# Cross- and self-attention layer: the maxima in one pair of banks with one VectorE instruction for each pair, and a third bank for the projections

## What is computed

```python
x = _layernorm(tgt, ln1_g, ln1_b)
qkv = x @ sa_wqkv
q, k, v = (_heads(t) for t in jnp.split(qkv, 3, axis=-1))
wei = jnp.einsum('bhtd,bhsd->bhts', q, k) * scale
wei = jnp.where(causal[None, None], wei, NEG_INF)
wei = jnp.where(tgt_padding_mask[:, None, None, :], NEG_INF, wei)
wei = jax.nn.softmax(wei, axis=-1)
sa_out = _merge(jnp.einsum('bhts,bhsd->bhtd', wei, v)) @ sa_wproj + sa_bproj
result = tgt + sa_out
xq = _layernorm(result, ln2_g, ln2_b)
xs = _layernorm(src, ln2_g, ln2_b)
kv = xs @ ed_wkv
k2, v2 = (_heads(t) for t in jnp.split(kv, 2, axis=-1))
q2 = _heads(xq @ ed_wq)
wei2 = jax.nn.softmax(jnp.einsum('bhtd,bhjd->bhtj', q2, k2) * scale, axis=-1)
ed_out = _merge(jnp.einsum('bhtj,bhjd->bhtd', wei2, v2)) @ ed_wproj + ed_bproj
result = result + ed_out
h = jax.nn.relu(_layernorm(tgt, ln3_g, ln3_b) @ ff_w1 + ff_b1)
result = result + (h @ ff_w2 + ff_b2)
```

## Time and profile before

| | |
|---|---|
| median of 3 runs | 609.78 us (607.84 to 613.45) |
| the profiled execution | 610.33 us |
| its span, first to last instruction | 608.3 us |
| mean granted TensorE clock | 0.979 of full speed |
| TensorE busy | 551.4 us (91%) |
| VectorE busy | 402.9 us (66%) |
| ScalarE busy | 330.6 us (54%) |
| GpSimd busy | 110.1 us (18%) |

### The profile page before, as it was taken

How to read it: one execution, slowest core, us unless ns; L and a number is a source line. 1 busy time by engine, 2 the same in 40 slices (tenths; PEclk the granted TensorE clock), 3 DMA queues, 4 the chain that set the end, 5 groups by cost and what they waited for, 6 DMA issues and landing times.

```text
span 608.3 us, 14162 instructions
## 1 busy us (share of the span) xinstructions
PE 551.4 (91%) x5564; PEld 445.1 (73%) x5564; DVE 402.9 (66%) x982; ACT 330.6 (54%) x615; POOL 110.1 (18%) x367
## 2 busy tenths in 40 slices
PE   3999877999999989899999999899999999999896
PEld 3887765768877877768877777768877777768674
DVE  7943767797477747696478747697568654685571
ACT  5626444266546746267546755357545665375183
POOL 2002312031023112031113112032113111130010
PEclk9869988999999999999999999999999999999998
DMA  8896077593650177392660168393570138104900
GB/s 234 172 133 121 20 118 112 84 116 70 121 123 1 46 107 114 69 127 57 121 135 6 46 84 122 66 123 62 115 119 13 32 81 135 35 3 89 125 2 16
DMA packets 74210, 52.84 MB, mean 87 GB/s; under 512 B 21984, under 2 KB 73376, under 8 KB 74144
## 3 DMA queue, kind: packets, MB, share of 16 engines
q1 hardware_dynamic: 74144, 51.94, 51.3%
HBM read 14.36 MB, written 1.84 MB: 27 GB/s over the span
## 4 chain that ended last, share of the span: by engine, by line
PE 72%; DVE 13%; ACT 8%; issue 3%; POOL 3%; DMA 1%; SPq 0%; DVEq 0%; POOLq 0%; ACTq 0%
PE misc L1142 9%; PE misc L978 9%; PE pvb L1113 9%; PE misc L980 7%; PE misc L979 7%; PE scb L1097 7%; PE mxb L1081 5%; PE misc L1149 5%; DVE negm L885 3%; DVE rem L819 2%; ACT prob L747 2%; PE misc L1120 2%; PE mxb L1078 2%; PE scb L1092 2%; PE misc L1034 2%
## 5 line engine op out<-in xcount | busy, mean ns | idle before, releaser
L747 ACT ACTIVATE prob<-scb 125x448 f32<-125x448 f32 (+1 forms) x256 | 134.8, 544 | 72.1 <-PE scb L1097 68.6
L885 DVE TENSOR_REDUCE negm<-mxb 112x1 f32<-112x375 f32 x256 | 129.4, 540 | 30.0 <-PE mxb L1081 28.8
L1081 PE MATMUL mxb<-k2st,q2st 96*112 96x375 bf16 x256 | 82.0, 338 | 5.7 <-DVE negm L885 5.4
L1097 PE MATMUL scb<-q2st,k2st 128*125 128x112 bf16 x768 | 74.7, 223 | 3.2 <-ACT prob L747 2.1
L1097 PEld LDWEIGHTS scb<-q2st,k2st 128*125 128x125 bf16 x768 | 65.7, 137 | 15.8 <-ACT prob L747 7.9
L819 DVE SCALAR_TENSOR_TENSOR rem<-misc,bcol,qkp 128x224 f32<-128x224 f32 (+2 forms) x64 | 37.5, 586 | 57.2 <-ACT qkp L732 57.0
L678 POOL CAST mparts<-negm 112x8 bf16<-112x8 f32 x64 | 12.5, 195 | 320.8 <-DVE negm L882 175.3
L1142 PE MATMUL misc<-wf,hT 128*112 128x256 f32 x256 | 60.6, 382 | 5.0 <-DVE rem L819 5.0
L1113 PE MATMUL pvb<-prob,v 125*17 125x112 f32 (+1 forms) x2048 | 65.0, 261 | 0.1
L732 ACT ACTIVATE qkp<-misc,bcol 128x224 bf16<-128x224 f32 (+2 forms) x64 | 35.8, 559 | 51.1 <-PE misc L980 51.1
L882 DVE TENSOR_REDUCE negm<-mxb 112x4 f32<-112x448 f32 x64 | 39.2, 616 | 29.1 <-PE mxb L1078 28.9
(11 more groups left out here) (150 smaller groups left out, 1160.6 us busy)
## 6 DMA issues: line engine op xcount, KB each, us to landing
k2st<-qkp SPq DMA_DIRECT2D x192, 93.8 KB, 4.3
xs<-in_ctx SPq DMA_DIRECT2D x16, 375.0 KB
q1st<-qkp SPq DMA_DIRECT2D x48, 112.0 KB, 5.2
k1st<-qkp SPq DMA_DIRECT2D x48, 112.0 KB, 6.6
q2st<-qkp SPq DMA_DIRECT2D x96, 56.0 KB, 2.3
xn<-in_x SPq DMA_DIRECT2D x4, 448.0 KB, 8.0
tb<-in_x SPq DMA_DIRECT2D x8, 224.0 KB, 10.6
out<-ostage SPq DMA_DIRECT2D x16, 112.0 KB, 3.7
```

The source lines that it names most:

```text
L747: nc.scalar.activation(prob[0:rows, n % PROB_SLOTS, :], scb[n % SCORE_BANKS][0:rows, 0:GH * T], ACT.Exp, scale=SCALE).then_inc(s_ex, 1)
L885: V.tensor_reduce(negm[:, at, i:i + 1], mx[0:T, 0:S], axis=AX_X, op=ALU.max, negate=True).then_inc(s_mx, 1)
L1081: mm = M(mx[0:T, 0:S], q2st[0:NROW, i, b * T:(b + 1) * T], k2st[k2_place(q, b)][0:NROW, i, 0:S], start=True, stop=True)
L1097: mm = M(sc[0:rows, j * T:(j + 1) * T], ks, (q1st if u < BG else q2st)[:, h, b * T:(b + 1) * T], start=(u >= BG), stop=(u >= BG or j == GH ...
```

## The change

The three banks `mxb0` to `mxb2` become one tensor `mxb` of two banks, and `misc` gets the third. A `max` step is now a pair: two heads of a cross unit, one in each bank, or twice four heads of a self unit. TensorE fills both banks and signals once; VectorE reduces both with one instruction, over 2 x 375 or 2 x 4 x 112 columns. TensorE's wait is for the reduce of the pair directly before. The quarters' lists follow: a quarter that had four cross maxima has two pairs; the self maxima of quarters g and g + 1 become one pair in the odd quarter, and `max_parts` follows as before.

```diff
-MISC_BANKS, MAX_BANKS, SCORE_BANKS = 2, 3, 2
+MISC_BANKS, SCORE_BANKS = 3, 2
...
     def maxima(u, g):
-        heads = [g] if u < BG else range(4 * g, 4 * g + 4)
-        return [[("max", u, i)] for i in heads] + ([[("max_parts", u, g // 2)]] if g % 2 else [])
+
+        pairs = range(2 * g, 2 * g + 2) if u >= BG else [g // 2] if g % 2 else []
+        return [[("max", u, i)] for i in pairs] + ([[("max_parts", u, g // 2)]] if g % 2 else [])
...
-    opening = [("v1", 0, 0), ("ff1", 0, 2 * kt), ("max", 0, 0, 0), ("max", 0, 0, 1), ("max_parts", 0, 0, 0), ("v1", 0, 1), ("ff1", 0, 2 * kt + 1),
-               ("mT", 0, 0, 0), ("v1", 0, 2), ("ff1", 0, 2 * kt + 2), ("max", 0, 0, 2), ("load_src", 0, 0), ("max", 0, 0, 3), ("max_parts", 0, 0, 1),
-               ("score", 0, 0, 0, 0), ("max", 0, 1, 0), ("score", 0, 0, 1, 0), ("max", 0, 1, 1), ("max_parts", 0, 1, 0), ("v1", 0, 3),
+    opening = [("v1", 0, 0), ("ff1", 0, 2 * kt), ("max", 0, 0, 0), ("max_parts", 0, 0, 0), ("v1", 0, 1), ("ff1", 0, 2 * kt + 1),
+               ("mT", 0, 0, 0), ("v1", 0, 2), ("ff1", 0, 2 * kt + 2), ("load_src", 0, 0), ("max", 0, 0, 1), ("max_parts", 0, 0, 1),
+               ("score", 0, 0, 0, 0), ("max", 0, 1, 0), ("score", 0, 0, 1, 0), ("max_parts", 0, 1, 0), ("v1", 0, 3),
                ("mT", 0, 0, 1), ("ff1", 0, 2 * kt + 3)]
...
-        mxb = [ps(f"mxb{i}", [P, 512]) for i in range(MAX_BANKS)]
+        mxb = ps("mxb", [P, 2, 512])
...
                     if u < BG:
-                        V.tensor_reduce(negm[:, at, i * GH:(i + 1) * GH], mx[0:T, 0:GH * T].rearrange("p (h s) -> p h s", h=GH),
-                                        axis=AX_X, op=ALU.max, negate=True).then_inc(s_mx, 1)
+                        into, of = negm[:, at, i * HH:(i + 1) * HH], mxb[0:T, :, 0:GH * T].rearrange("p a (h s) -> p a h s", h=GH)
                     else:
-                        V.tensor_reduce(negm[:, at, i:i + 1], mx[0:T, 0:S],
-                                        axis=AX_X, op=ALU.max, negate=True).then_inc(s_mx, 1)
+                        into, of = negm[:, at, 2 * i:2 * i + 2], mxb[0:T, :, 0:S]
+                    V.tensor_reduce(into, of, axis=AX_X, op=ALU.max, negate=True).then_inc(s_mx, 1)
...
-                    after(pe, s_mx, before_in(maxes, s, MAX_BANKS))
-                    m, first = divmod(i * (GH if u < BG else 1), HH)
+                    after(pe, s_mx, before_in(maxes, s, 1))
+                    m, first = divmod(i * (HH if u < BG else 2), HH)
...
+                    for a in range(2):
+                        mx = mxb[:, a, :]
+                        if u < BG:
...
+                            for j in range(GH):
+                                h = i * HH + a * GH + j
...
+                        else:
+                            h = 2 * i + a
+                            mm = M(mx[0:T, 0:S], q2st[0:NROW, h, b * T:(b + 1) * T], k2st[k2_place(q, b)][0:NROW, h, 0:S], start=True, stop=True)
                     mm.then_inc(s_mxf, 1)
```

More of the change, by code:

```diff
@@ L367, in layer_kernel @@
         misc = [ps(f"misc{i}", [P, 512]) for i in range(MISC_BANKS)]
-        mxb = [ps(f"mxb{i}", [P, 512]) for i in range(MAX_BANKS)]
+        mxb = ps("mxb", [P, 2, 512])
         scb = [ps(f"scb{i}", [P, 512]) for i in range(SCORE_BANKS)]
         pvb = ps("pvb", [P, 512])
-        qk_bank, vcol_bank, col_bank, row_bank, f1_bank = scb[0], scb[1], pvb, scb[0], mxb[0]
+        qk_bank, vcol_bank, col_bank, row_bank, f1_bank = scb[0], scb[1], pvb, scb[0], mxb[:, 0, :]
         s_w = [sem(f"{w}_landed") for w in ("wqkv", "wkv", "wq2", "wff1")]
@@ L675, in pool_part @@
                     parts = mparts[n % 2]
-                    after(pool, s_mx, ("max", q, u, 2 * half + 1 if u < BG else (half + 1) * HH - 1))
+                    after(pool, s_mx, ("max", q, u, half if u < BG else (half + 1) * HH // 2 - 1))
                     after(pool, s_full, before_in(halves, ("mT", q, u, half), 2))
@@ L875, in dve_part @@
                     u, i = s[2:]
-                    mx = mxb[maxes.index(s) % MAX_BANKS]
                     at = units.index((q, u)) % 2
@@ L1072, in pe_part @@
                         after(pe, s_k2st[b][m], ("stack_k2", q, b, m))
[L1073 to L1081, removed]
+                    for a in range(2):
+                        mx = mxb[:, a, :]
+                        if u < BG:
+                            M(mx[0:T, 0:GH * T].rearrange("p (h s) -> p h s", h=GH), maskt[:, b, :],
+                              identb[0:T, :].unsqueeze(1).broadcast_to([T, GH, T]), start=True, stop=False)
+                            for j in range(GH):
+                                h = i * HH + a * GH + j
+                                mm = M(mx[0:T, j * T:(j + 1) * T], q1st[0:NROW, h, b * T:(b + 1) * T], k1st[0:NROW, h, b * T:(b + 1) * T],
+                                       start=False, stop=(j == GH - 1))
+                        else:
+                            h = 2 * i + a
+                            mm = M(mx[0:T, 0:S], q2st[0:NROW, h, b * T:(b + 1) * T], k2st[k2_place(q, b)][0:NROW, h, 0:S], start=True, stop=True)
                     mm.then_inc(s_mxf, 1)
```

## The result

The changed kernel takes 638.8 us (median of four runs, 636.53 to 639.49) against 608.8 us before: 1.046 times as long, 95% interval 1.041 to 1.050. The direction was forecast, the size not: 30 us where 13 were forecast, above the range's end at 636. The kernel before was timed again beside the experiments, with medians of 609.5, 610.5 and 610.1 us, so a difference between two kernels of different sets is good to a us or two.

What follows compares the result with a forecast made beforehand. TensorE's in-order stream, busy 91% of the span, was taken as the bound. 50 us lost at pairs less 37 taken away (24 third `misc` bank, 6 mT, 7 old `mxb` waits) gave +13 on 609.78: 623 us, range 606 to 636.

Steps and rivals of the forecast that it cites:

- The cycle: From one maxima pair's fill to the next: fill, VectorE start, reduce of 0.93 us, release; 1.51 us in all.
- the sum: The forecast's account over the whole kernel: 50 us lost on pairs less 37 us taken away, +13 us.
- the third `misc` bank: Removes TensorE's waits for readers of misc banks: 22 us (11 to 32) plus 2 us at the ends, 24.
- Rival (a): Break-even, 611 us, chance 0.27: late reduce and misc bank wait share one cause and can't both be paid.
- The ring's rows behind the 22: 20 lines of TensorE load waits for misc bank readers, 95 to 580 us: 32.1 us in 65 waits, taken as 22.
- Of the four groups: 4 x 12.1: Stalls at cross pairs: 7.0 us a group from little work between, 5.1 from late VectorE; 48 us over four groups.
- the 1.19 us: Part of the 1.51 us from pair to pair that must be filled with other TensorE work.
- The self pairs cost nothing: Self pairs come once in two quarters, over 5 us of TensorE work apart, covering their 1.5 us; cost nothing.
- 10 to 24: VectorE time saved, in us, by 160 reduces instead of 320; counts only where a matmul waits behind VectorE's queue.
- Rival (b): Faster, 599 us, chance 0.1: VectorE's queue is the hidden pacer and its full 24 us come back.
- Rival (c): Worse, 635 us, chance 0.13: each of 60 pairs costs 0.2 us more, +12, as stalls push VectorE's work back.
- The rule that was weighed: Rotate matmul groups through banks; break up unsaturated VectorE's instructions where it causes bubbles. By it alone, +37 us.

## Why the prediction was right or wrong

**Right: what a pair costs where it stalls.** The cycle was put at 1.51 us and is 1.51 to 1.56. The reduce was put at 0.93 us and is 0.935. The waits of one group (119.39 to 262.30 us) in the changed kernel:

```profile
PE mxb L1082 <- DVE negm L885: 9.4, 15, 1.5
PE scb L1098 <- ACT prob L748: 2.5, 6, 0.6
```

9.4 us in 15 waits, and with the 0.17 us by which a matmul's row outlasts the distance to the next one (0.33 less 0.16), 15 x 0.17 = 2.5 more, is 11.9 us; the sum had 12.1 for a group, at 15 places. The long one was named too: 1.50 us at the second pair of (3, 3), put at 1.7.

**Right in total, in part by luck: the third `misc` bank.** Put at 24, measured 24.3 with pairs and 18.0 without. Rival (a), that it can't be paid beside the stalls, falls with it. In the traces the steady part gives 19.2 us, not 22, and the start 7.9, not 2. The start's share is unsure: kernels with the same steps up to there reach the first group's unit 3 at 91.44 and 93.59 us with three banks and at 99.34 and 96.24 with two, so it is 3 to 8 us. The ring's rows behind the 22 also lack one of 1.0 us (L978 for `xsT_lo`). mT's matmuls waited 4.7 us for `mparts` and now wait 1.0, where the sum took 6 off.

**Wrong: "Of the four groups: 4 x 12.1".** This is the step that failed by most. The end of the last group was costed like any other. There, the order is the same but the fillers are of a group that doesn't exist, so the work that fills the 1.19 us isn't there; nor are there ring waits to be gained. The end and the last unit 3 lose 16.4 us together, against 8 for two steady groups; up to the last unit 3 the traces are only 9.8 us apart, where the forecast's 13 us would have made about 9. Spreading unit 6's maxima takes 7.2 of it away, and keeping TensorE at work shows that part of it is clock, which no term of the sum held.

**Wrong: "The self pairs cost nothing".** The cover named was the distance from one self pair to the next. The next user of the banks behind the self pair of (2, 3) is a cross pair, 0.39 us of TensorE's work later. The kernels with and without self pairs are 7 us apart, of which the stricter wait at the first maximum of a cross unit has a part (0.45 us a group where it was seen).

**Left out: what stood between the score tiles.** A step of maxima was also what separated two score tiles, long enough for the exponential to free a bank of `scb`. With half as many steps, the tiles wait: 2.5 us a group in matmul rows, 8.2 us in all by the kernel with three score banks.

**Too small, the other way:** one instruction in place of two was given no worth of its own, and the kernel that undoes it is 11 us slower (5 to 18), of which about 5 are seen in stretches of equal clock. It was in the sum only inside the cycle. And VectorE's busy time was forecast near 379 us and is 395.5: the 150 ns fixed in a reduce's duration mostly lie under its neighbour, as the spacing of 0.45 us in the earlier trace rows had shown, so 24 us was the wrong end of "10 to 24".

Added to the 37 us that the sum had for pairs without a third bank, the 7 for self pairs and 8 for score tiles make 52, against 53.6 measured. That the books close so nearly is chance: the end's clock and the missing fillers stand in no term, and these terms overlap. By place, the trace with pairs and two `misc` banks loses 8.6 us in the start (another kernel with the same steps loses 5.4 there), 10.5 in each of two groups, 7.2 in the next up to its unit 3, and 16.4 in the last unit 3 and the end. Shown is that each effect exists and what the time falls by when it alone is taken away.

Rival (b), that VectorE's saved time comes back, was wrong in size: 11 us by the ratios, not 24. Rival (c), 635 us, came nearest to 638.8, for another reason: its later reduces would show in every steady group, and these lose 4.0 us against 3.2.

The rule that was weighed, the Trainium skill, Perfetto Trace Analysis, sections Matmuls and Optimizing Scalar/DVE Operations, is borne out in its half on rotation: making one unrotated pair of two single banks cost 37.0 us, and giving up the third bank of the ring 16.6, together 53.6 before the freed bank gave 24 back. Its sum of +37, for a third bank of no worth, is to be set beside these 53.6. The half on breaking up instructions is not borne out by itself: at 62% VectorE was not saturated, yet two reduces in place of one, on the same single buffer, made the kernel slower; the page says only that breaking up may help.

No version was found that clearly beats both kernels. The nearest is the kernel before with its third bank of maxima given to `misc`, at 0.9974 of its time.

## What to carry to other kernels

When two buffers are merged so that one instruction can read both, count the cycle of filling, reading and release, and look for the work that stands between two fills at every place of the program: at its end, where fillers run out, and where another kind of step uses the same buffer next. A step that is moved or merged was also a spacer: ask which other ring it gave time to. And price a bank by what each ring gives for it; here one bank was worth 18 us in one ring and 17 in the other, so moving it was free. What cost was to fill, read and wait for the two banks left to the maxima as one; the single instruction over both, taken alone, saved time.

## What the runs showed of the hardware

A wait of 2.94 us and further waits of 1.03 us between pairs of matmuls were followed by a granted clock of 0.57 from 585 to 597 us, and sixteen ff2 matmuls took 6.26 us. In the kernel with two `misc` banks, three waits of 1.03 us in a row came before the 0.58 of 616 to 623 us, and the same matmuls took 6.12; with five more matmuls in each such wait the clock stayed at 1.00 and they took 3.62. In the steady groups of the changed kernel waits of 0.3 to 1.5 us, each with other matmuls between, left it at 1.00. That is not always so. In the kernel with the extra matmuls at its end, unit 1 of the third group had a granted clock of 0.64 from 336 to 340.7 us, after waits of 0.84 and 0.35 us, and took 16.03 us; with the same steps in the groups before and behind it took 15.07, at 1.00. In the kernel with self pairs and single cross maxima, a wait of 2.53 us before 316.97 was followed by 0.58 from 317.3 to 321.3.

One VectorE reduce can read two PSUM banks: 750 columns in two banks take 935 ns and 375 columns in one take 540 ns, so the second bank costs its columns at 1.05 ns each and nothing more.
